# One 256-column matmul for the first layer of the edge network, and a second bank for the edge sums

## The reference

```python
h = relu(layernorm(x))
s, v = h[:, :64], h[:, 64:].reshape(n, 32, 3)
xs = s @ W1_s / 8;  xv = einsum('nmc,mk->nkc', v, W1_v) / sqrt(32)
w = silu(edge_embed @ fc_w1 + fc_b1) @ fc_w2 + fc_b2      # 8 -> 64 -> 192 per edge
m0_a = w[:, :64] * xs[src] * sh0                            # and three more products of
m1_a = (w[:, 64:128] * xs[src])[:, :, None] * sh1[:, None]  # w, the gathered row and sh
agg = segment_sum(msg, dst, n) / sqrt(0.5)
out = agg_s @ W2_s / sqrt(96) + s @ Wsc_s / 8               # and the same for the vectors
x + h + concat(silu(out[:, :64]), out_v * silu(out[:, 64:96]))
```

## Time and profile before

| | us |
|---|---|
| median of 3 runs | 825.63 |
| lowest and highest | 825.25, 831.32 |
| the profiled execution | 822.46 |
| its span, first to last instruction | 820.8 |

### The profile page before, as it was taken

How to read it: one execution, slowest core, us unless ns; L and a number is a source line. 1 busy time by engine, 2 the same in 40 slices (tenths; PEclk the granted TensorE clock), 3 DMA queues, 4 the chain that set the end, 5 groups by cost and what they waited for, 6 DMA issues and landing times.

```text
span 820.8 us, 16769 instructions
## 1 busy us (share of the span) xinstructions
PE 648.3 (79%) x5900; PEld 544.9 (66%) x5900; DVE 348.5 (42%) x1126; ACT 183.8 (22%) x357; POOL 405.1 (49%) x434
## 2 busy tenths in 40 slices
PE   6656776877797797797789789779778978977877
PEld 6535665666676686686577668668667766866766
DVE  7412444433454443444345434434343443444435
ACT  4611112212121212112212212121221221212121
POOL 2374555545554644554554455545556455544630
PEclk9755556555655555555555555555555555555657
DMA  9621111112111211211211211112212121111210
GB/s 297 165 71 41 52 49 53 46 50 57 48 49 49 65 40 49 63 41 49 57 44 48 53 48 52 52 42 57 56 46 54 45 57 48 49 53 44 57 39 13
DMA packets 38783, 48.10 MB, mean 59 GB/s; under 512 B 9908, under 2 KB 31443, under 8 KB 38379
## 3 DMA queue, kind: packets, MB, share of 16 engines
q0 software_dynamic: 20160, 34.33, 15.8%
q1 hardware_dynamic: 18193, 13.46, 5.5%
q10 hardware_dynamic: 410, 0.07, 0.1%
HBM read 40.67 MB, written 4.00 MB: 54 GB/s over the span
## 4 chain that ended last, share of the span: by engine, by line
PE 59%; another core or an unknown queue 17%; issue 11%; DVE 7%; DVEq 1%; ACT 0%; ACTq 0%
PE ps L701 20%; PE ps L691 15%; PE ps L682 7%; PE ps L696 7%; PE ps L733 3%; PE ps L697 2%; DVE agg L592 2%; DVE P L555 2%; PE ps L726 2%; PE ps L731 1%; PE ps L727 1%; PE ps L673 1%; DVE M L535 1%; DVEq L577 1%
## 5 line engine op out<-in xcount | busy, mean ns | idle before, releaser
L463 POOL DMA_INDIRECT gath<-table,src_sb x416 | 396.4, 953 | 362.1 <-DVE P L555 255.2
L701 PE MATMUL ps<-S,P 128*64 128x32 f32 x2496 | 294.7, 289 | 60.6 <-issue 60.1
L701 PEld LDWEIGHTS ps<-S,P 128*64 128x64 f32 x2496 | 273.2, 218 | 67.3 <-issue 66.8
L696 PE MATMUL ps<-S,P 128*64 128x48 f32 x832 | 180.9, 317 | 55.4 <-DVE agg L592 53.8
L696 PEld LDWEIGHTS ps<-S,P 128*64 128x64 f32 x832 | 122.3, 206 | 102.7 <-DVE agg L592 60.2
L691 PE MATMUL ps<-fc_sb,hid 64*128 64x192 f32 x832 | 180.8, 557 | 9.1 <-issue 8.6
L697 PE MATMUL ps<-S,P 128*64 128x16 f32 x832 | 148.2, 256 | 10.1 <-issue 10.1
L496 ACT ACTIVATE hid<-ps,fb_sb 128x256 f32<-128x256 f32 x104 | 49.4, 475 | 450.0 <-PE ps L682 294.9
L691 PEld LDWEIGHTS ps<-fc_sb,hid 64*128 64x128 f32 x832 | 121.2, 311 | 43.4 <-issue 42.6
L550 DVE TENSOR_TENSOR P<-ps,gath 128x512 f32<-128x512 f32 x103 | 71.0, 690 | 167.8 <-PE ps L691 63.0
L697 PEld LDWEIGHTS ps<-S,P 128*64 128x64 f32 x832 | 136.5, 222 | 6.1 <-issue 5.6
(11 more groups left out here) (90 smaller groups left out, 260.9 us busy)
## 6 DMA issues: line engine op xcount, KB each, us to landing
gath<-table,src_sb POOLq DMA_INDIRECT x416, 3.5
agg<-zeros SPq DMA_DIRECT2D x3, 1024.0 KB, 12.4
emb<-emb_t SPq DMA_DIRECT2D x104, 24.0 KB
out<-res SPq DMA_DIRECT2D x24, 78.1 KB
x_sb<-x SPq DMA_DIRECT2D x5, 350.0 KB
table<-prod SPq DMA_DIRECT2D x3, 420.0 KB
sh_sb<-sh_t SPq DMA_DIRECT2D x1, 840.0 KB, 8.0
table<-prod SPq DMA_DIRECT2D x1, 280.0 KB
```

The costliest lines, as they stand in the source:

```text
L463: nc.gpsimd.indirect_dma_start(gath[:, u, j, :], None, table, bass.IndirectOffsetOnAxis(ap=src_sb[:, t:t + 1], axis=0)).then_inc(landed, 16)
L696: nc.tensor.matmul(oj[0:64, :, 0:3], pj[:, 64:128], sj[:, :, 1:4], start=True, stop=True)
L701: ins = nc.tensor.matmul(oj[64:128, :, c:4:3 - c], pj[:, lo:lo + 64], sj[:, :, 0:2 + c:1 + c], start=(c == 0), stop=(c == NC - 1), skip_gr ...
```

## The change

The two row tiles of the hidden layer become one. The host lays the 16 rows of both pairs of edge tiles next to each other, so a group's embedding is 16 rows by 256 columns at partition 0, and one matmul writes 256 columns into bank 0. ScalarE reads these 256 columns out of one bank. Bank 1 is free and takes the sums of every odd group; the even ones stay in bank 6. So `scatter` of group q waits until the sums of q-2 have been added, no longer those of q-1, and the special case for the last but one group goes. The last group's fourth tile goes to bank 1 instead of 6, the last node tile's output to bank 0 instead of 1. The block diagonal matrix is loaded with two DMAs instead of four.

```diff
-        fc1_sb = sb("fc1_sb", [32 + 2 * NB, 2 * HID])
-        emb = sb("emb", [32 + 2 * NB, SLOTS, TE])
+        fc1_sb = sb("fc1_sb", [2 * NB, 2 * HID])
+        emb = sb("emb", [2 * NB, SLOTS, 2 * TE])
         fb1_sb = sb("fb1_sb", [2 * HID, 1])
         fc2_sb = sb("fc2_sb", [2 * HID, WN])
         fb2_sb = sb("fb2_sb", [128, WN])
...
             (w_v_in[:, 1, :], wscv.unsqueeze(1).broadcast_to([V0, NC, V0])),
         ]
         other_loads = [
-            (fc1_sb[g:g + NB, 0:HID], fc1) for g in (0, 32)] + [(fc1_sb[g + NB:g + 2 * NB, HID:], fc1) for g in (0, 32)] + [
+            (fc1_sb[0:NB, 0:HID], fc1), (fc1_sb[NB:, HID:], fc1),
             (fb1_sb[0:HID, :], fb1), (fb1_sb[HID:, :], fb1), (fc2_sb[0:HID, :], fc2), (fc2_sb[HID:, :], fc2),
             (fb2_sb[:, :], fb2.broadcast_to([128, WN])),
             (wo_v[:, :], w2v), (wo_s[0:S0, :], w2s[0:S0, :]), (wo_s[96:128, :], w2s[S0:96, :]),
...
         pass_sems = p_emb + p_gath + p_last + [p_prime, p_seed, p_M, p_hidps, p_hid, p_w, p_prod, p_S, p_out, p_agg, p_win,
                                       n_cols, n_ps, n_act, n_xh, n_gate, n_res, n_out]
-
-        def hid_ps(g):
-            return ps[:, g, 0:TE]
-
-        hid_both = ps[:, 0:2, 0:TE]
+        hid_ps = ps[:, 0, 0:2 * TE]
 
         def w_ps(u):
             return ps[:, 2 + 2 * (u % 2):4 + 2 * (u % 2), :].rearrange("p b (j w) -> p (b j) w", j=2)
-        def out_ps(q):
-            bank = 0 if isinstance(q, int) and q == NQ - 2 else 6
-            return ps[:, bank, 0:QT * WIN * AC].rearrange("p (j n c) -> p j n c", j=QT, c=AC)
+        def out_ps(u):
+            return ps[:, 6 - 5 * (u % 2), 0:QT * WIN * AC].rearrange("p (j n c) -> p j n c", j=QT, c=AC)
 
         def last_ps(j):
             lo = WIN * AC * (j % 2) * (j < 2)
-            return ps[:, (2, 2, 3, 6)[j], lo:lo + WIN * AC].rearrange("p (n c) -> p n c", c=AC)
-
-
-        o_ps = [ps[0:NTN, 7, 0:WN], ps[0:NTN, 7, 0:WN], ps[0:NTN, 1, 0:WN]]
+            return ps[:, (2, 2, 3, 1)[j], lo:lo + WIN * AC].rearrange("p (n c) -> p n c", c=AC)
+
+
+        o_ps = [ps[0:NTN, 7, 0:WN], ps[0:NTN, 7, 0:WN], ps[0:NTN, 0, 0:WN]]
 
         def of(t):
             return 0 if not isinstance(t, int) or t < NN - 2 else t - (NN - 3)
...
                         q = i * SLOTS + u
                         if not (isinstance(i, int) and i == 0):
                             sp.wait_ge(p_hidps, q - SLOTS + 1)
-                        sp.dma_start(emb[:, u, :], emb_t[:, bass.ds(q * TE, TE)]).then_inc(p_emb[u], 16)
+                        sp.dma_start(emb[:, u, :], emb_t[:, bass.ds(q * 2 * TE, 2 * TE)]).then_inc(p_emb[u], 16)
 
                     def store(t):
                         sp.wait_ge(n_res, t + 1)
...
                         act.wait_ge(p_hidps, q + 1)
                         if not (isinstance(i, int) and q < 2):
                             act.wait_ge(p_w, q - 1)
-                        nc.scalar.activation(hid[:, u % 2, :, :], hid_both, ACT.Silu, bias=fb1_sb[:, 0:1]).then_inc(p_hid, 1)
+                        nc.scalar.activation(hid[:, u % 2, :, :].rearrange("p g e -> p (g e)"), hid_ps, ACT.Silu, bias=fb1_sb[:, 0:1]).then_inc(p_hid, 1)
 
                         if isinstance(i, int) and i == 0 and u < 2:
                             act.wait_ge(p_prime, 2 * u + 2)
...
                             if not (isinstance(q, int) and q == 0 and j == 0):
                                 dve.wait_ge(p_agg, q * QT + j)
                             a = agg[:, bass.ds(cols[j], WIN * AC)]
-                            nc.vector.tensor_tensor(a, out_ps(q)[:, j, :, :].rearrange("p n c -> p (n c)"), a,
+                            nc.vector.tensor_tensor(a, out_ps(u)[:, j, :, :].rearrange("p n c -> p (n c)"), a,
                                                     ALU.add).then_inc(p_agg, 1)
 
                     def last_add(j, col):
...
                         pe.wait_ge(p_emb[u], (i + 1) * 16)
                         if not (isinstance(q, int) and q < 1):
                             pe.wait_ge(p_hid, q)
-                        for g in range(2):
-                            r = slice(32 * g, 32 * g + 2 * NB)
-                            ins = nc.tensor.matmul(hid_ps(g), fc1_sb[r, :], emb[r, u, :], start=True, stop=True)
-                        ins.then_inc(p_hidps, 1)
+                        nc.tensor.matmul(hid_ps, fc1_sb[:, :], emb[:, u, :], start=True, stop=True).then_inc(p_hidps, 1)
 
                     def weights(q, u):
                         pe.wait_ge(p_hid, q + 1)
...
                     def scatter(q, u):
                         pe.wait_ge(p_prod, q + 1)
                         pe.wait_ge(p_S, q + 1)
-                        if isinstance(q, int) and q == NQ - 2:
-                            pe.wait_ge(p_hid, NQ)
-                        elif not (isinstance(q, int) and q < 1):
-                            pe.wait_ge(p_agg, q * QT)
+
+                        if not (isinstance(q, int) and q < 2):
+                            pe.wait_ge(p_agg, q * QT - QT)
                         for j in range(QT):
-                            ins = scatter_tile(P[:, u % 2, j, :], S[:, u % 2, j, :, :], out_ps(q)[:, j, :, :])
+                            ins = scatter_tile(P[:, u % 2, j, :], S[:, u % 2, j, :, :], out_ps(u)[:, j, :, :])
                         ins.then_inc(p_out, 1)
 
                     def last_scatter(j):
...
     dst = np.pad(a["dst"], (0, pad), mode="edge")
     sh = np.pad(a["edge_attr_4"], ((0, pad + QT * TE), (0, 0)))
-    emb = np.pad(a["edge_attr_8"], ((0, pad), (0, 0))).reshape(NQ, 2, 2, TE, NB).transpose(2, 1, 4, 0, 3)
-    emb = np.pad(emb.reshape(2, 2 * NB, NQ * TE), ((0, 0), (0, 32 - 2 * NB), (0, 0))).reshape(64, NQ * TE)[:32 + 2 * NB]
+    emb = np.pad(a["edge_attr_8"], ((0, pad), (0, 0))).reshape(NQ, 2, 2, TE, NB).transpose(1, 4, 0, 2, 3)
+    emb = emb.reshape(2 * NB, NQ * 2 * TE)
     p = "L0_gnn_"
     arrays = {
         "x": a["x"],
```

## The result

| | median us | lowest to highest | runs |
|---|---|---|---|
| before | 825.44 | 823.17 to 831.32 | 4 |
| after | 837.75 | 831.44 to 838.15 | 4 |

The changed kernel takes 1.0159 times as long, 95% interval 1.0091 to 1.0226: slower by 1.6%, where the forecast was 836 us. Whether it is slower by more than 2% the interval leaves open. The profiled execution took 837.97 us, its span is 836.3.

The account below looks back on a forecast made before the run. TensorE was taken as the bound, with waits for adds and slowdowns beside long gather runs. Profiled 822.5 us + 38.6 for the longer matmul - 28.6 for the freed bank = 832.5, median 836; range 806 to 868 (8 in 10).

Parts of the forecast that it names:

- The bound: TensorE, busy 79% of the span, bounds an undisturbed group at 5.02 us; waits and slowdowns make up the rest.
- slow stretches: Times when TensorE starts one or two instructions every 0.7 us, inferred from eight gathers without pause; 6.1 to 6.7 us each.
- The stream: Hidden layer on TensorE: one 256-column matmul takes 1.15 us instead of 0.73, adding 38.6 us (34.0 to 43.4).
- 78 x 0.425: Hidden layers lasting 0.80 us, 78 of 104, each counted with the full 0.425 us of added columns.
- The bank: Scatter on TensorE no longer waits for the previous group's adds: 28.6 us gained of 53.8 (ends 0 and 53.8).
- rival (a): All 53.8 us of scatter waits come back, scatter starting before VectorE's release: 807.3 us, median 810; chance 0.20.
- Value taken: 13 x 1.69 + 6.6 = 28.6 us: Scatter waits for adds: 1.69 us recovered from each of 13 long gaps, plus 6.6 us from 11 short ones.
- Rival (b): Earlier products join GpSimd's gather runs: three runs of eight per eight groups instead of two, median 880 us; chance 0.20.
- (c): Longer step of 5.45 us opens pauses between gathers, parting half the loop's 20 long runs: median 792 us; chance 0.10.
- (d): Second bank of sums buys nothing, freed scatter waits or loses the time next step: 861 us, median 864; chance 0.12.
- (e): Fewer gaps and more columns bring TensorE to 2.4 GHz, then gathers bound: 583 us; chance 0.03.

Follow-up runs that it names:

- The run: Changed kernel with all sums back in bank 6, 256-column matmul kept, on the third chip: 829.95 us, 1.0009 times the kernel before.

## Why the prediction was right, point by point

**The bound.** "Here TensorE is the bound", said of an undisturbed group, holds for that group and does not carry the sum. The slow stretches were read rightly as following runs of eight gathers, and the kernels with pauses bear out that long runs cause them on the chips where they occur: the longer the pause, the less is lost. That the runs are not enough by themselves I had not seen: on the second chip one run of 416 gathers held nothing. The SBUF page of the Trainium skill (SBUF — State Buffer, Who interferes with whom) says that a DMA never contends with a compute engine; by that, pauses in the gathers could only cost time. The second chip agrees (+23%), the others do not (-13% for the same kernel on the third, and 711 us for the changed one on the fifth).

**The stream.** The slot was forecast at 1.15 us and measured at 1.15; the group at 5.44 and measured at 5.44. The term, +38.6 us, was wrong: 2 us on the third chip, with an interval of -3 to +4 (0.9968 to 1.0050 times 828). The step that failed is "78 x 0.425": it counts every undisturbed slot in full, as if TensorE were the bound wherever it has no gap. The run shows that nearly all of these 0.42 us were covered; the row at 327.25 shows one place where they were, by a release that was seen later anyway.

**The bank.** -28.6 us, in truth +43 on the third chip. The waits did go (53.8 to 0 for TensorE's matmuls), and the scatter did run inside the slow stretch, before VectorE's release, which the prediction had set as the sign of rival (a). But the step "Value taken: 13 x 1.69 + 6.6 = 28.6 us" asks only what a wait is worth to the engine that waits, and puts what follows from its end into a rival.

**Rival (b)** is what happened, by its mechanism, and further than it was priced: products sooner after a release, two runs of four joined, four runs of eight per eight groups, not three. Its price per run was too high for the new state. Eight groups take 60.2 us after (runs of gathers that begin at 225.47 and at 285.69), and 60.2 - 8 x 5.44 - 2 x 2.65 = 11.4, so 2.8 us for each of four runs instead of 6.1 to 6.7 for each of two: TensorE now works inside the stretch. What sets the eight groups is the loop of 15.06 us, four times over. So 836 us is luck: two errors that cancel on the first chip and not on the third. +38.6 - 28.6 = +10 was forecast, about 2 + 43 was measured on the third, and on the first, where the two parts were not measured by themselves, 2 + 10 if the stream costs 2 there too. A chance of 0.35 for that sum was too high and 0.20 for (b) too low.

**Rivals (c) to (e).** (c), that a longer step parts the runs, is the opposite of what came. (d), 864 us, comes near the third chip's 873, for another reason. (e) did not come: the trace of the kernel after has a mean clock of 0.55. The 583 us that (e) gives with the gathers as the bound are near what the kernel before takes on the second chip (578). Without gathers the clock there was 1.00 from 200 us on, with a busy share of 86%, where 82% went with 0.50 in the earlier trace rows.

**What stays open.** Why one of the chips doesn't hold releases, and runs the same program in 578 us. The gathers themselves are no slower on the others: their last DMA packet ends 2.2 to 2.3 us after their start on every chip (medians from 200 to 450 us). The granted clock is a second difference that goes with the first. The kernel before has a mean of 0.64 to 0.70 on the second chip and 0.53 to 0.57 on the others, and the 588 us that the prediction adds up from TensorE's slots at the lower clock would not fit into 578 us. With the pause the second chip has 0.53 to 0.54 too and takes 712 us. Which of the two comes first is not shown. Why TensorE's weights come later on the third chip than on the first is open; whether one bank would gain the same on the first chip, and whether another bank than bank 1 would do the same as it, wasn't tried. And by what the gathers hold TensorE's increments.

## What to carry to other kernels

Before a wait is taken away, follow what its end starts, once around the loop: here the wait for the adds kept the products apart and so the gathers in runs of four, and taking it away cost 43 us on one chip although 88 us of TensorE's waiting went with it. Where a profile shows work that is over but seen late, look for the engine that issues without a pause at that time, and test it by adding idle work there: 153 us of memset made this kernel 13% faster on the third chip. And a per cent or two should be timed on more than one chip, since 1.6% on one was 5.6% on another, and what gained 13% on one cost 23% on another.

## What the runs showed of the hardware

- Gathers from GpSimd, 1.25 us apart (0.95 and 0.30), without a pause for more than some 5 us, go, in the traces of the first, third and fourth chip, with releases that VectorE and ScalarE see up to 2 us after the last gather's end (a wait of 6.77 us in the rows of the kernel after) and with TensorE starting its instructions 0.7 us apart. It is the record of TensorE's increments that is late: 5.9 us for the scatter that ended at 216.06. No trace of the fifth chip has such a run, but the kernel before takes as long there. On the second chip none of TensorE's 208 increments for hidden layers and weights was over 0.03 us late in one run of 416 gathers.
- A pause of 0.73 us in such a run did not end it: in the earlier trace rows the release still came at 225.12, some 1.5 us after the last gather's end. One of 1.23 us brings the kernel before to 769 to 785 us, 1.48 to 739, 1.65 to 718 (on three chips whose times for the unaltered kernel agree within 0.4%).
- One core's time for the same program was 578 us on one chip and 825 to 828 on the four others, while the last DMA packet of a gather ended 2.2 to 2.3 us after its start on all five.
- TensorE, in f32: one matmul of 256 columns has a slot of 1.15 us at the lower clock, two of 128 columns in two row tiles 0.73.
